# A fused attention and expert layer on one core: the buffers in on-chip memory allocated in another order, by 128-byte phase

## The chip, the cores and the metric

The kernel runs on one core of a Trainium2 chip. The metric is the device time of one execution in microseconds. The core's engines are named as in the profile: PE is TensorE (matmul), PEld its weight loads, DVE is VectorE, ACT is ScalarE, POOL is GpSimd, SP is SyncE, which issues the DMAs.

## The reference: what is computed

For a batch of 8 sequences of 1024 tokens with 256 channels:

```
# attention
qkv = x @ Wqkv + bqkv;  q, k, v = split(qkv)
q2 = (q - mean(q))**2;  q2 = q2 / (sum(q2) + 1e-7);  q2 = l2norm(q2, channels)
k2 = (k - mean(k))**2;  k2 = k2 / (sum(k2) + 1e-7);  k2 = l2norm(k2, tokens)
kv = einsum('bnc,bnd->bcd', k2, v)
t2 = einsum('bnc,bcd->bnd', q2, kv) / sqrt(N)
x  = layernorm(x + (v + t2) @ Wln + bln)
# experts: 16 experts of 128 hidden channels, all of them for every token
sel    = sigmoid(einsum('bsd,ed->bse', x, expert_sel))
scores = relu(einsum('bsd,edh->bseh', x, keys))
x  = layernorm(x + einsum('bseh,ehv,bse->bsv', scores, values, sel))
```

All of it is float32.

## The kernel before

**Precision.** An operand of a large product is kept as two tensors of the type float32r, a high part (`_h`) and a low part (`_l`). `product` makes one product from three matmuls, high by high, high by low, and low by high. In the profile all of these have line L956.

**Tiling.** Tokens go in 8 tiles of 128 for each batch element, in two halves of four tiles (512 tokens). A step belongs to one expert and one half, so there are 32 steps for each batch element, and 256 in all. In each step PE does, in this order:

- *up*: `up_bank`, hidden scores of one expert for 512 tokens. Six matmuls with 512 columns. Stationary are slices of `keys_h` and `keys_l`; moving are slices of `x1T_h` and `x1T_l` (the layer's middle result, transposed).
- what the tables `LOOP`, `FIRST` and `LAST` plan for this step, from the attention of the next batch element: *QK* (`qk_bank`, six matmuls of 512 columns, stationary `xT`, moving `wqk`), *GG* (`g_bank`, six of 256, stationary `x_h`/`x_l`, moving `k2_h`/`k2_l`), *Y* (`ring_bank`, twelve of 256, stationary `xT` and `qT`, moving `wvl` and `kvw`), *KV* (twelve of 256, stationary `gT`, which is the same memory as `k2_h`/`k2_l`, moving `wvl`), *LG* (four of 512, stationary `esel`, moving `x1T`), the transposes *QT* and *XT* (stationary `q2` or `x1`, moving `ident`, 128 columns) and the small sums *KS*.
- *down*: `down_bank`, the product with `vals`, for the gated scores of the step before. Twelve matmuls of 256 columns, stationary slices of `gated_h`/`gated_l`, moving `vals_h`/`vals_l`.

DVE makes `gated` from `up_bank` (L932) and its low part (L938), ACT the high part. The order on every engine is written out in the kernel; nothing reorders it.

**Memory.** `sb(...)` (L136 on) allocates a tensor in the on-chip memory. The allocator places tensors one behind another in the order of the calls, each rounded up to a multiple of 32 bytes per partition. All matmul operands are float32 or float32r, so 4 bytes a column. Inside a tensor, the slices that matmuls read begin at multiples of 512 bytes, so the address of a slice modulo 128 is that of its tensor. This remainder is called *phase* here.

Of the kernel before, what the change touches and what calls it, by code (L numbers as in the profile page):

```python
# [6 lines left out]
F32R = mybir.dt.float32r  # L7
# [4 lines left out]
P = 128  # L12
B, N, C = 8, 1024, 256
E, H = 16, 128
M = C // P
T = N // P
GT = 4
GN = GT * P
G = T // GT
STEPS = G * E  # L20
LAG = 1
WARM = 14
LOW = 32
EPS_SUM = 1e-7
EPS_NORM = 1e-12
# [98 lines left out]
def build_program(nc, x, xT, wqk, wvT, wln, b_qk, b_v, b_ln, esel, keys, values, ident_in, out):  # L124
    with ExitStack() as ctx:
        def sb(name, shape, dt=F32):
            return ctx.enter_context(nc.sbuf_tensor(name, shape, dt))
# [4 lines left out]
        def sem(name):  # L132
            return ctx.enter_context(nc.semaphore(name))


        keys_h, keys_l = sb("keys_h", [P, E, M, H], F32R), sb("keys_l", [P, E, M, H], F32R)  # L136
        vals_h, vals_l = sb("vals_h", [P, E, C], F32R), sb("vals_l", [P, E, C], F32R)
        wqk_h, wqk_l = sb("wqk_h", [P, M, 2 * C], F32R), sb("wqk_l", [P, M, 2 * C], F32R)
        wvl_h, wvl_l = sb("wvl_h", [P, M, C], F32R), sb("wvl_l", [P, M, C], F32R)

        esel_h, esel_hl = sb("esel_h", [P, M, P], F32R), sb("esel_hl", [P, M, P], F32R)
        qk_bias = sb("qk_bias", [P, 2 * C])
        bvl = sb("bvl", [P, C])
        out_bias = sb("out_bias", [P, C])
        ident = sb("ident", [P, P])
        ones = sb("ones", [P, P])
        eps_ln = sb("eps_ln", [P, 1])


        x_raw = sb("x_raw", [P, T, C])  # L150
        xT_raw = sb("xT_raw", [P, M, GN])
        xT_h, xT_l = sb("xT_h", [P, G, M, GN], F32R), sb("xT_l", [P, G, M, GN], F32R)
        x_h, x_l = sb("x_h", [P, 2, C], F32R), sb("x_l", [P, 2, C], F32R)
        qk = sb("qk", [P, 2 * C])
        q2 = sb("q2", [P, T, C])
        q_sum, q4_sum, q_root, q_floor, q_scale = (sb(n, [P, T]) for n in (
            "q_sum", "q4_sum", "q_root", "q_floor", "q_scale"))
        q4_lifted = sb("q4_lifted", [P, T])
        k2, k4 = sb("k2", [P, 2, C]), sb("k4", [P, C])
        k_sum, k_sum_eps, k_scale = (sb(n, [P, 2]) for n in ("k_sum", "k_sum_eps", "k_scale"))  # L160
        k2_h, k2_l = sb("k2_h", [P, 2, C], F32R), sb("k2_l", [P, 2, C], F32R)
        k2_total, k4_total = sb("k2_total", [P, C]), sb("k4_total", [P, C])
        col_sums = sb("col_sums", [P, 4, 2])
        col_norm, col_scale = sb("col_norm", [P, M, 2]), sb("col_scale", [P, M, 2])
        gT_h, gT_l = k2_h, k2_l
        kvw_h, kvw_l = sb("kvw_h", [P, M, C], F32R), sb("kvw_l", [P, M, C], F32R)
        qT_h, qT_l = sb("qT_h", [P, 2, 2, M, P], F32R), sb("qT_l", [P, 2, 2, M, P], F32R)
        y = sb("y", [P, 2, C])
        y_stats, y_mv = sb("y_stats", [P, 2, 6]), sb("y_mv", [P, 2, 2])
        y_std, y_rstd = sb("y_std", [P, 2]), sb("y_rstd", [P, 2])  # L170
        kvw = y
        x1 = sb("x1", [P, T, C])
        x1T_h, x1T_l = sb("x1T_h", [P, G, M, GN], F32R), sb("x1T_l", [P, G, M, GN], F32R)


        sel = sb("sel", [E, GN])
        sel_rows = sb("sel_rows", [P, E // 4, GN])
        sel_all = sb("sel_all", [P, 2, GN])
        gated = sb("gated", [P, GN])
        gated_h, gated_l = sb("gated_h", [P, 2, GN], F32R), sb("gated_l", [P, 2, GN], F32R)  # L180
        w_room = sb("w_room", [P, WPIECE])
        z = sb("z", [P, 2, 2, C])
        z_stats, z_mv = sb("z_stats", [P, 2, 2, 6]), sb("z_mv", [P, 2, 2, 2])
        z_std, z_rstd, z_shift = (sb(n, [P, 2, 2]) for n in ("z_std", "z_rstd", "z_shift"))


        w_stage = [w_room[:], z[:].rearrange("p a t c -> p (a t c)")]
# [2 lines left out]
        wqk_flat = wqk_raw.rearrange("p m a c -> p (m a) c")  # L190
        wqk_hi_flat = wqk_h[:].rearrange("p m (a c) -> p (m a) c", a=2)
        wqk_lo_flat = wqk_l[:].rearrange("p m (a c) -> p (m a) c", a=2)
        minus_mean, bias_mean = sb("minus_mean", [P, 2 * M]), sb("bias_mean", [P, 2])
        bqk_raw = sel_all[:, 0].rearrange("p (a c) -> p a c", a=2)
        bln_raw = y[:, 1]
        bv_col = sb("bv_col", [P, M])
        bv_wide = y[:, 0].rearrange("p (m n) -> p m n", m=M)
        table_ahead = sb("table_ahead", [P, 2])
        esel_raw = sb("esel_raw", [P, M, E])


        up_bank = [bank("up_bank0"), bank("up_bank1")]
# [60 lines left out]
        def at_least(eng, sm, count):  # L263

            if not isinstance(count, int) or count > 0:
                eng.wait_ge(sm, count)
# [20 lines left out]
        def ring_of(it, s, kind, a):  # L287
            rep = it if isinstance(it, int) else 1
            return ring_bank[RING_AT[(rep, s, kind, a)] % 2]
# [194 lines left out]
        def _(act):  # L484
            def copy(dst, src, **kw):
                return nc.scalar.activation(dst, src, ACT.Copy, **kw)  # L486
# [78 lines left out]
            def late(it, s):  # L565
# [6 lines left out]
                for kind, a, off in transposed_first(  # L572
# [32 lines left out]
                    elif kind == "LG":  # L605
# [5 lines left out]
                        at_least(act, sel_spread, b * STEPS + a * E - (E - 1))  # L611
                        copy(sel[:], ring_of(it, s, kind, a)[LOW:LOW + E, :]).then_inc(logits_low, 1)
                    elif kind == "ZN":
# [32 lines left out]
        def _(dve):  # L646
# [34 lines left out]
            def wvl_esel_lo():  # L681
# [8 lines left out]
                dve.wait_ge(esel_hi, 1)  # L690
                V.tensor_tensor(esel_hl[:, :, LOW:LOW + E], esel_raw[:], esel_h[:, :, 0:E].bitcast(F32),
                                ALU.subtract).then_inc(esel_lo, 1)
# [254 lines left out]
        def _(pe):  # L947
# [31 lines left out]
            pe.wait_ge(constants_set, 4)  # L979
            for n in range(WARM):  # L980
                mm(ring_bank[n % 2][:, 0:M * P], ones[:], esel_h[:].bitcast(F32).rearrange("p m n -> p (m n)"),  # L981
# [174 lines left out]
```

## Time and profile before

| | |
|---|---|
| median of 3 runs | 1044.8 us (1041.42 to 1045.15) |
| profiled execution, own time | 1044.54 us |
| its span in the trace | 1042.7 us |
| PE busy | 1019.5 us, 98% |
| PEld busy | 924.3 us, 89% |
| DVE busy | 796.7 us, 76% |
| ACT busy | 509.3 us, 49% |
| POOL busy | 220.1 us, 21% |
| mean DMA traffic | 31 GB/s |

The span runs from the first to the last instruction; the own time holds about 1.8 us around it. A matmul's duration in the profile holds its latency through the array, so durations of neighbours overlap, and their sum is far above the time that passes; how fast PE goes is read from starts, or from the chain that ended last, which follows PE from start to start and merges matmuls of one kind (x12 is twelve of them).

### The profile page before, as it was taken

The page shows a single profiled execution, that of the slowest core. Times are in us where ns is not written, and L with a number is a line of the kernel's source. Part 1 is how long each engine was busy: PE and PEld are TensorE (multiplying, and loading weights), DVE is VectorE, ACT ScalarE, POOL GpSimd, SP SyncE. Part 2 cuts the span into 40 slices and gives each one's busy share as a digit, 9 for nine tenths or more (in the row PEclk, how much of TensorE's full clock was granted, in tenths as well). Part 3 has the DMA queues.
Part 4 walks back from the last instruction along what each step waited for, and adds up shares of the span by engine and source line. Part 5 has one row for each costly group of instructions (what it writes and reads, how often), then busy time and mean ns, then how long its engine had stood idle before and what let it go on. Part 6 is the DMA issues. An engine that isn't in the chain of part 4 may idle for free.

```text
span 1042.7 us, 18409 instructions
## 1 busy us (share of the span) xinstructions
PE 1019.5 (98%) x6664; PEld 924.3 (89%) x6664; DVE 796.7 (76%) x1818; ACT 509.3 (49%) x1192; POOL 220.1 (21%) x273
## 2 busy tenths in 40 slices
PE   7789999999999999999999999999999999999997
PEld 6669899988999899998999989998999988999986
DVE  7779786878778787778877778677786878877565
ACT  6555653455534654356534565245643455434332
POOL 2111122212222122221222122221121211221221
PEclk9889999999999999999999999999999999999999
DMA  5032000110002000110001100011000200000000
GB/s 179 21 102 82 2 22 1 63 41 3 21 13 72 20 2 22 42 61 2 2 21 43 61 3 21 1 53 51 2 22 1 83 21 3 22 2 21 2 21 21
DMA packets 12122, 32.59 MB, mean 31 GB/s; under 512 B 1792, under 2 KB 2048, under 8 KB 12032
## 3 DMA queue, kind: packets, MB, share of 16 engines
q1 hardware_dynamic: 12032, 31.42, 9.0%
q8 instruction: 53, 0.87, 0.3%
q14 instruction: 37, 0.30, 0.1%
HBM read 22.50 MB, written 8.39 MB: 30 GB/s over the span
## 4 chain that ended last, share of the span: by engine, by line
PE 96%; DVE 3%; ACT 1%; issue 1%; POOL 0%; ACTq 0%; POOLq 0%
PE down_bank L956 34%; PE up_bank L956 34%; PE ring_bank L956 10%; PE qk_bank L956 8%; PE g_bank L956 4%; PE ring_bank L1044 1%; PE ring_bank L1060 1%; PE ring_bank L981 1%; PE ring_bank L1069 1%; PE ring_bank L1070 1%; PE ring_bank L1025 1%; DVE keys_l L909 0%; DVE k_l L852 0%; DVE qk L720 0%; DVE k_total L849 0%
## 5 line engine op out<-in xcount | busy, mean ns | idle before, releaser
L486 ACT ACTIVATE gated_h<-gated 128x512 fp32r<-128x512 f32 x256 | 161.4, 630 | 403.2 <-DVE gated L932 403.2
L472 POOL PARTITION_BROADCAST sel_all<-sel_rows x240 | 197.0, 821 | 710.2 <-DVE gated L932 709.5
L956 PE MATMUL down_bank<-vals_h,gated_h 128*128 128x256 f32 x1024 | 291.9, 285 | 0.9 <-DVE gated_l L938 0.8
L956 PE MATMUL down_bank<-vals_l,gated_h 128*128 128x256 f32 x1024 | 285.2, 279 | 0.0
L956 PE MATMUL down_bank<-vals_h,gated_l 128*128 128x256 f32 x1024 | 285.2, 279 | 0.0
L932 DVE SCALAR_TENSOR_TENSOR gated<-up_bank,sel_all 128x512 f32<-128x512 f32 x256 | 176.1, 688 | 63.0 <-PE up_bank L956 61.7
L938 DVE TENSOR_TENSOR gated_l<-gated,gated_h 128x512 fp32r<-128x512 f32 x256 | 173.3, 677 | 43.5 <-ACT gated_h L486 42.5
L956 PE MATMUL up_bank<-x1T_h,keys_l 128*128 128x512 f32 x512 | 202.4, 395 | 0.0
L956 PE MATMUL up_bank<-x1T_l,keys_h 128*128 128x512 f32 x512 | 201.9, 394 | 0.0
L956 PEld LDWEIGHTS down_bank<-vals_h,gated_h 128*128 128x128 f32 x1024 | 193.2, 189 | 9.3 <-DVE gated_l L938 3.2
L956 PE MATMUL up_bank<-x1T_h,keys_h 128*128 128x512 f32 x512 | 201.2, 393 | 0.0
L956 PEld LDWEIGHTS down_bank<-vals_l,gated_h 128*128 128x128 f32 x1024 | 192.9, 188 | 4.6
L956 PEld LDWEIGHTS down_bank<-vals_h,gated_l 128*128 128x128 f32 x1024 | 192.7, 188 | 0.0
L956 PEld LDWEIGHTS up_bank<-x1T_h,keys_l 128*128 128x128 f32 x512 | 96.7, 189 | 20.4
L956 PEld LDWEIGHTS up_bank<-x1T_l,keys_h 128*128 128x128 f32 x512 | 96.8, 189 | 11.5
L956 PEld LDWEIGHTS up_bank<-x1T_h,keys_h 128*128 128x128 f32 x512 | 96.7, 189 | 11.1
L720 DVE TENSOR_TENSOR qk<-qk_bank,qk_bias 128x512 f32<-128x512 f32 x60 | 41.3, 689 | 35.9 <-PE qk_bank L956 35.8
L733 DVE TENSOR_TENSOR y<-ring_bank,x_raw 128x256 f32<-128x256 f32 x64 | 27.0, 423 | 32.9 <-PE ring_bank L956 32.9
L956 PE MATMUL qk_bank<-wqk_h,xT_h 128*128 128x512 f32 x120 | 49.1, 409 | 0.0
L956 PE MATMUL qk_bank<-wqk_h,xT_l 128*128 128x512 f32 x120 | 47.4, 395 | 0.0
L956 PE MATMUL qk_bank<-wqk_l,xT_h 128*128 128x512 f32 x120 | 47.3, 394 | 0.0
L486 ACT ACTIVATE k_h<-k,k_scale 128x256 fp32r<-128x256 f32 x64 | 32.6, 509 | 27.8 <-DVE k_scale L767 27.1
(158 smaller groups left out, 1682.0 us busy)
## 6 DMA issues: line engine op xcount, KB each, us to landing
xT_raw<-in_xT SPq DMA_DIRECT2D x16, 512.0 KB, 4.0
x_raw<-in_x SPq DMA_DIRECT2D x16, 512.0 KB, 4.6
out<-z SPq DMA_DIRECT2D x32, 256.0 KB, 2.3
w_room<-in_keys SPq DMA_DIRECT2D x4, 512.0 KB, 4.3
z<-in_values SPq DMA_DIRECT2D x4, 512.0 KB, 3.8
sel_rows<-sel SPq DMA_DIRECT2D x64, 8.0 KB
x<-in_wqk SPq DMA_DIRECT2D x1, 512.0 KB, 3.6
sel_all<-in_b_qk SPq DMA_DIRECT2D x1, 256.0 KB, 5.1
```

The costliest lines, as they stand in the source:

```text
L472: nc.gpsimd.partition_broadcast(sel_all[:, e % 2], row, P).then_inc(sel_spread, 1)
L486: return nc.scalar.activation(dst, src, ACT.Copy, **kw)
L720: V.tensor_tensor(qk_of(it, t)[:], qk_bank_of(it, t)[:], qk_bias[:], ALU.add).then_inc(qk_biased, 1)
L733: V.tensor_tensor(y[:, a % 2], ring_of(it, s, "Y", a)[:, 0:C], x_raw[:, a], ALU.add).then_inc(y_added, 1)
L932: V.scalar_tensor_tensor(out=gated[:], in0=up_bank[s % 2][:], scalar=0.0, in1=sel_all[:, s % 2], op0=ALU.max, op1=ALU.mult).then_inc(gate_ ...
L938: V.tensor_tensor(gated_l[:, s % 2], gated[:], gated_h[:, s % 2].bitcast(F32), ALU.subtract).then_inc(gated_lo, 1)
L956: last = mm(dst, lhs, rhs, start=start and i == 0, stop=stop and i == n - 1, **kw)
L981: mm(ring_bank[n % 2][:, 0:M * P], ones[:], esel_h[:].bitcast(F32).rearrange("p m n -> p (m n)"), start=True, stop=True)
L1025: last = mm(bk[:, j:j + 2], total[:, m * P:(m + 1) * P], ones[:, 0:2], start=True, stop=True)
L1044: last = nc.tensor.transpose(bk[:, j:j + P], q2[:, 2 * a + i, m * P:(m + 1) * P], ident[:])
L1060: last = nc.tensor.transpose(bk[:, m * P:(m + 1) * P], x1[:, a, m * P:(m + 1) * P], ident[:])
L1069: mm(bk[:], esel_hl[:, m], x1T_h[:, a, m], start=(m == 0), stop=False)
```

## The change

The `sb` calls stand in another order. Moving operands come first, then 64 bytes that nothing uses (`half_line`), then stationary operands, then everything that no matmul reads, with small tensors (under 128 bytes) at the end. No shape, no instruction and no wait is changed; on each engine the same instructions stand in the same order, and only the addresses in them differ. The core of the diff:

```diff
+LINE = 128
...
-        keys_h, keys_l = sb("keys_h", [P, E, M, H], F32R), sb("keys_l", [P, E, M, H], F32R)
         vals_h, vals_l = sb("vals_h", [P, E, C], F32R), sb("vals_l", [P, E, C], F32R)
+        x1T_h, x1T_l = sb("x1T_h", [P, G, M, GN], F32R), sb("x1T_l", [P, G, M, GN], F32R)
         wqk_h, wqk_l = sb("wqk_h", [P, M, 2 * C], F32R), sb("wqk_l", [P, M, 2 * C], F32R)
         wvl_h, wvl_l = sb("wvl_h", [P, M, C], F32R), sb("wvl_l", [P, M, C], F32R)
...
+        kvw_h, kvw_l = sb("kvw_h", [P, M, C], F32R), sb("kvw_l", [P, M, C], F32R)
+        k2_h, k2_l = sb("k2_h", [P, 2, C], F32R), sb("k2_l", [P, 2, C], F32R)
+        gT_h, gT_l = k2_h, k2_l
+        ident, ones = sb("ident", [P, P]), sb("ones", [P, P])
+
+
+        half_line = sb("half_line", [P, LINE // 8])
+        keys_h, keys_l = sb("keys_h", [P, E, M, H], F32R), sb("keys_l", [P, E, M, H], F32R)
+        gated_h, gated_l = sb("gated_h", [P, 2, GN], F32R), sb("gated_l", [P, 2, GN], F32R)
         xT_h, xT_l = sb("xT_h", [P, G, M, GN], F32R), sb("xT_l", [P, G, M, GN], F32R)
         x_h, x_l = sb("x_h", [P, 2, C], F32R), sb("x_l", [P, 2, C], F32R)
+        qT_h, qT_l = sb("qT_h", [P, 2, 2, M, P], F32R), sb("qT_l", [P, 2, 2, M, P], F32R)
+        esel_h, esel_hl = sb("esel_h", [P, M, P], F32R), sb("esel_hl", [P, M, P], F32R)
+        q2, x1 = sb("q2", [P, T, C]), sb("x1", [P, T, C])
+        k2_total, k4_total = sb("k2_total", [P, C]), sb("k4_total", [P, C])
```

Phases (address modulo 128) in the two built programs, moving / stationary, for each kind of product:

| product | matmuls in one batch element | before | after |
|---|---|---|---|
| up: `x1T` / `keys` | 192 of 512 columns | 64 / 0 | 0 / 64 |
| down: `vals` / `gated` | 384 of 256 | 0 / 64 | 0 / 64 |
| QK: `wqk` / `xT` | 48 of 512 | 0 / 32 | 0 / 64 |
| GG: `k2` / `x_h`, `x_l` | 48 of 256 | 64 / 32 | 0 / 64 |
| Y, first half: `wvl` / `xT` | 48 of 256 | 0 / 32 | 0 / 64 |
| Y, second half: `kvw` / `qT` | 48 of 256 | 32 / 32 | 0 / 64 |
| KV: `wvl` / `gT` | 12 of 256 | 0 / 64 | 0 / 0 |
| LG: `x1T` / `esel` | 8 of 512 | 64 / 0 | 0 / 64 |
| transposes: `ident` / `q2`, `x1` | 32 of 128 | 0 / 32, 0 / 64 | 0 / 64 |

## Rows read from the trace of the kernel before

**Rows 1.** The page: busy time by engine, and slices of PE and its clock.
```profile
PE 1019.5 (98%) x6664; PEld 924.3 (89%) x6664; DVE 796.7 (76%) x1818; ACT 509.3 (49%) x1192; POOL 220.1 (21%) x273
...
PE   7789999999999999999999999999999999999997
...
PEclk9889999999999999999999999999999999999999
```

**Rows 2.** The page: the chain that ended last, by engine.
```profile
PE 96%; DVE 3%; ACT 1%; issue 1%; POOL 0%; ACTq 0%; POOLq 0%
```

**Rows 3.** Stretches of one batch element: us, busy of PE, PEld, DVE, ACT, POOL (instructions), clock, DMA.
```profile
287.00:412.00 125.00, 125.00 (x833) 113.95 (x833) 97.92 (x226) 62.48 (x148) 26.41 (x33) 1.00 0.08 27
412.00:537.00 125.00, 125.00 (x833) 113.95 (x832) 97.87 (x227) 62.48 (x148) 26.34 (x32) 1.00 0.08 27
```

**Rows 4.** PE's waits, 100 to 1036 us: in total, times, longest.
```profile
PE down_bank L956 <- DVE gated_l L938: 0.8, 1, 0.8
```

**Rows 5.** The chain in order of time, 442 to 566.7 us: start, length, what.
```profile
442.00 1.50 PE down_bank L956 x12
443.51 1.40 PE up_bank L956 x6
444.91 1.42 PE ring_bank L956 x12
446.33 1.36 PE down_bank L956 x12
447.69 1.37 PE up_bank L956 x6
449.06 1.39 PE down_bank L956 x12
...
466.44 1.41 PE down_bank L956 x12
467.85 1.40 PE up_bank L956 x6
...
469.47 1.40 PE qk_bank L956 x6
470.87 1.42 PE down_bank L956 x12
472.28 1.40 PE up_bank L956 x6
473.69 0.70 PE g_bank L956 x6
474.39 1.42 PE down_bank L956 x12
475.80 1.40 PE up_bank L956 x6
...
563.07 0.44 PE ring_bank L1044 x4
563.50 1.39 PE down_bank L956 x12
564.89 1.37 PE up_bank L956 x6
```

**Rows 6.** The chain a little later, 479 to 505 us.
```profile
483.00 1.40 PE qk_bank L956 x6
484.39 1.38 PE down_bank L956 x12
485.77 1.37 PE up_bank L956 x6
487.14 0.71 PE g_bank L956 x6
```

**Rows 7.** The longest pieces of the whole chain that repeat once a batch element.
```profile
566.70 1.50 PE down_bank L956 x12
...
691.40 1.50 PE down_bank L956 x12
```

More of the change, by code:

```diff
@@ L133, in sem @@
             return ctx.enter_context(nc.semaphore(name))
-        keys_h, keys_l = sb("keys_h", [P, E, M, H], F32R), sb("keys_l", [P, E, M, H], F32R)
         vals_h, vals_l = sb("vals_h", [P, E, C], F32R), sb("vals_l", [P, E, C], F32R)
+        x1T_h, x1T_l = sb("x1T_h", [P, G, M, GN], F32R), sb("x1T_l", [P, G, M, GN], F32R)
         wqk_h, wqk_l = sb("wqk_h", [P, M, 2 * C], F32R), sb("wqk_l", [P, M, 2 * C], F32R)
         wvl_h, wvl_l = sb("wvl_h", [P, M, C], F32R), sb("wvl_l", [P, M, C], F32R)
-        esel_h, esel_hl = sb("esel_h", [P, M, P], F32R), sb("esel_hl", [P, M, P], F32R)
@@ L142, in build_program @@
[L142 to L151, printed above, removed]
+        kvw_h, kvw_l = sb("kvw_h", [P, M, C], F32R), sb("kvw_l", [P, M, C], F32R)
+        k2_h, k2_l = sb("k2_h", [P, 2, C], F32R), sb("k2_l", [P, 2, C], F32R)
+        gT_h, gT_l = k2_h, k2_l
@@ L154, in build_program @@
+        esel_h, esel_hl = sb("esel_h", [P, M, P], F32R), sb("esel_hl", [P, M, P], F32R)
+        q2, x1 = sb("q2", [P, T, C]), sb("x1", [P, T, C])
+        k2_total, k4_total = sb("k2_total", [P, C]), sb("k4_total", [P, C])
+        x_raw, xT_raw = sb("x_raw", [P, T, C]), sb("xT_raw", [P, M, GN])
+        qk_bias = sb("qk_bias", [P, 2 * C])
+        bvl, out_bias = sb("bvl", [P, C]), sb("out_bias", [P, C])
         qk = sb("qk", [P, 2 * C])
-        q2 = sb("q2", [P, T, C])
-        q_sum, q4_sum, q_root, q_floor, q_scale = (sb(n, [P, T]) for n in (
-            "q_sum", "q4_sum", "q_root", "q_floor", "q_scale"))
@@ L158, in build_program @@
-        q4_lifted = sb("q4_lifted", [P, T])
         k2, k4 = sb("k2", [P, 2, C]), sb("k4", [P, C])
[L160 to L165, printed above, removed]
@@ L166, in build_program @@
-        kvw_h, kvw_l = sb("kvw_h", [P, M, C], F32R), sb("kvw_l", [P, M, C], F32R)
-        qT_h, qT_l = sb("qT_h", [P, 2, 2, M, P], F32R), sb("qT_l", [P, 2, 2, M, P], F32R)
         y = sb("y", [P, 2, C])
-        y_stats, y_mv = sb("y_stats", [P, 2, 6]), sb("y_mv", [P, 2, 2])
-        y_std, y_rstd = sb("y_std", [P, 2]), sb("y_rstd", [P, 2])
         kvw = y
-        x1 = sb("x1", [P, T, C])
-        x1T_h, x1T_l = sb("x1T_h", [P, G, M, GN], F32R), sb("x1T_l", [P, G, M, GN], F32R)
         sel = sb("sel", [E, GN])
@@ L179, in build_program @@
         gated = sb("gated", [P, GN])
-        gated_h, gated_l = sb("gated_h", [P, 2, GN], F32R), sb("gated_l", [P, 2, GN], F32R)
         w_room = sb("w_room", [P, WPIECE])
         z = sb("z", [P, 2, 2, C])
+        eps_ln = sb("eps_ln", [P, 1])
+        q_sum, q4_sum, q_root, q_floor, q_scale = (sb(n, [P, T]) for n in (
+            "q_sum", "q4_sum", "q_root", "q_floor", "q_scale"))
+        q4_lifted = sb("q4_lifted", [P, T])
+        k_sum, k_sum_eps, k_scale = (sb(n, [P, 2]) for n in ("k_sum", "k_sum_eps", "k_scale"))
+        col_sums = sb("col_sums", [P, 4, 2])
+        col_norm, col_scale = sb("col_norm", [P, M, 2]), sb("col_scale", [P, M, 2])
+        y_stats, y_mv = sb("y_stats", [P, 2, 6]), sb("y_mv", [P, 2, 2])
+        y_std, y_rstd = sb("y_std", [P, 2]), sb("y_rstd", [P, 2])
         z_stats, z_mv = sb("z_stats", [P, 2, 2, 6]), sb("z_mv", [P, 2, 2, 2])
         z_std, z_rstd, z_shift = (sb(n, [P, 2, 2]) for n in ("z_std", "z_rstd", "z_shift"))
+        minus_mean, bias_mean = sb("minus_mean", [P, 2 * M]), sb("bias_mean", [P, 2])
+        bv_col, esel_raw = sb("bv_col", [P, M]), sb("esel_raw", [P, M, E])
+        table_ahead = sb("table_ahead", [P, 2])
         w_stage = [w_room[:], z[:].rearrange("p a t c -> p (a t c)")]
@@ L192, in build_program @@
         wqk_lo_flat = wqk_l[:].rearrange("p m (a c) -> p (m a) c", a=2)
-        minus_mean, bias_mean = sb("minus_mean", [P, 2 * M]), sb("bias_mean", [P, 2])
         bqk_raw = sel_all[:, 0].rearrange("p (a c) -> p a c", a=2)
         bln_raw = y[:, 1]
-        bv_col = sb("bv_col", [P, M])
         bv_wide = y[:, 0].rearrange("p (m n) -> p m n", m=M)
-        table_ahead = sb("table_ahead", [P, 2])
-        esel_raw = sb("esel_raw", [P, M, E])
         up_bank = [bank("up_bank0"), bank("up_bank1")]
```

## The prediction

> **What bounds the kernel now.** I read the page first. PE is busy for 98% of the span, DVE for 76%, the rest far less [rows 1], and the chain that ended last is PE for 96% of its length, DVE for 3% [rows 2]. In the stretches of one batch element PE is busy for all of the 125 us at full clock, 2.4 GHz [rows 3]. From 100 to 1036 us PE waits for another engine only once, for 0.8 us [rows 4]. So outside the first 66 us or so nobody holds PE up, and its time is the sum of the distances from one matmul's start to the next.
>
> These distances are in the chain. Pure streaming at 2.4 GHz would take 256/2.4 = 106.7 ns for a matmul of 256 columns and 213.3 ns for one of 512, so 1.28 us for a group of twelve down matmuls and also for a group of six up matmuls. The chain shows neither. It shows two paces: a quick one, 1.36 us for down and 1.37 us for up (446.33 and 447.69), and a slow one, 1.42 us and 1.40 us (470.87 and 472.28, 474.39 and 475.80) [rows 5]. Per matmul that is 113 or 118 ns for 256 columns, and 228 or 233 ns for 512. Same instructions, same shapes, same addresses modulo 128, no wait in either. Of the 32 down groups between 442.0 and 566.7 us, 20 take 1.36 to 1.39 us, eleven 1.41 or 1.42, and one, behind a transpose, 1.50; the 32 together are 44.68 us. Of the 32 up groups, 21 take 1.37 or 1.38 and eleven 1.40; together 44.18 us. The pace carries over from a group to the next: 470.87 to 475.80 is slow in all of its up and down groups, 446.33 to 447.69 quick [rows 5]. One period is 124.70 us, 566.70 to 691.40 [rows 7], and there are close to eight of them in the span, so a microsecond per period is worth 8 us.
>
> **The change part by part.** No instruction is added, removed or moved, on any engine or queue. What can change is how long PE takes to read its operands, and how long the others take to read and write theirs.
>
> *Products whose phases differ by 32 or 0 now and by 64 after* (QK, GG, Y). In the same stretch the eight QK groups take 1.40 us each, never 1.37 [rows 5, 6]. The nine groups of twelve in the ring (eight Y and one KV) take 12.72 us, so 1.413 each, as 1.42 at 444.91 [rows 5]. The eight GG groups take 5.79 us, one of them 0.81, the others 0.70 to 0.72 [rows 5, 6]; twelve at that pace would be 1.42. So all products that are not 64 apart go at the slow pace or close to it, and those that are 64 apart, up and down, at the quick pace two times in three. I read that as a connection, though not a proven one. If the former go as up and down do on average (down 44.56/32 = 1.393 without the transposed one's extra 0.12, up 1.381), Y and KV gain 9 x 0.020 = 0.18 us, GG 8 x (0.724 - 0.697) = 0.22, QK 8 x 0.019 = 0.15: 0.55 us a period.
>
> *Up and down, 64 apart before and after.* What is left is where the slow pace starts. Behind GG, down is slow (473.69, then 474.39); behind Y it is quick (444.91, then 446.33), behind QK either (469.47 then 1.42, 483.00 then 1.38) [rows 5, 6]. If GG and QK no longer stand apart, some of the eleven slow groups of each kind become quick. All of them would give 11 x 0.055 + 11 x 0.03 = 0.94 us, with the mixed groups of 1.38 and 1.39 brought to 1.36 as well 32 x 1.36 + 0.12 = 43.64 against 44.68 and 32 x 1.37 = 43.84 against 44.18, so 1.38 us. None gives 0. I take half of the 1.38, 0.7 us, as nothing says which neighbours stay slow: transposes remain, with `x1` at the phase it had.
>
> *KV* goes from 64 apart to 0 apart, the one product that goes the other way: twelve matmuls a period, at most 0.06 us a period if it is slow after, as the difference of 1.42 and 1.36. LG is only mirrored, eight matmuls a period; I put it at nothing.
>
> *Other engines.* DVE, ACT, POOL and the DMAs get other addresses too, all still multiples of 32 bytes. I cost that at nothing, because DVE has 27 us of slack in each 125 us [rows 3] and PE waits for it nowhere [rows 4]. Without cover, in the first 66 us and the last few, DVE is 3% of the chain [rows 2], 31 us; a change of one per cent in its speed would be 0.3 us.
>
> The sum is 0.55 + 0.7 - 0.06 = 1.2 us a period, times eight 9.5 us. The profiled execution's own 1044.5 us becomes 1035.0; the median of the runs is 0.3 us above it. I predict **1035 us**.
>
> The bounds of this term from rows: everything at the quick pace saves 1.38 us for up and down, 9 x 0.053 = 0.48 for the ring, 8 x (0.724 - 0.68) = 0.35 for GG and 8 x 0.03 = 0.24 for QK, 2.45 us a period, 20 us in all: **1025 us**. Everything at the slow pace costs 32 x 1.42 + 0.12 - 44.68 = 0.88 for down and 32 x 1.40 - 44.18 = 0.62 for up, 1.5 us a period: **1057 us**.
>
> **The rivals.**
>
> *Phase does not matter.* The two paces come out of the timing of the loads and matmuls alone, and come out alike. For it: the same phases show both paces [rows 5], which an address alone cannot make. Against it: QK, GG and Y never show the quick one. The time is that of before, 1044.8 us. The Trainium skill speaks for this rival, and against any gain: its page "SBUF — State Buffer", section "Who interferes with whom", gives TensorE two independent read ports, one for the moving operand and one for the weights, and says that "PE and ACT never wait on anyone". The trace agrees as to other engines, in that PE has no wait in the steady part [rows 4], but by that rule alone the chain should show one pace and not two.
>
> *The mirrored phase is worse, or everything locks at the slow pace* (the other side). Up is the only large product whose moving phase changes, from 64 to 0. The one product of 512 columns whose moving operand stands at phase 0 now, QK, takes 1.40 us in all eight groups and never 1.37 [rows 5, 6]. If that is because of its moving phase, the 21 quick up groups go to 1.40, 0.62 us a period, 5 us: 1050 us, and since the pace carries over, down would follow at 1.42, which is the 1057 us above. It decides from the point where up alone is slow, if the other products gain nothing. Against it: GG's moving operand is at 64 and is no quicker than Y's at 0.
>
> *A third pace, free of all loss.* If reading both operands at once is what keeps PE above 106.7 ns, and a distance of 64 everywhere removed it, the pace would be that of the transposes. Four of them take 0.44 us for 4 x 128 columns [rows 5], at two cycles a column 106.7 ns each, so 3.3 ns above pure streaming. One period has some 780 matmuls of the large products, whose pure streaming takes 109 us (40.96 for down, as much for up, 11.5 for the ring, 10.2 for QK, 5.1 for GG, less rounding) and which take 118.6 now (44.68 + 44.18 + 12.72 + 11.20 + 5.79); with 3.3 ns each, 2.6 us, 7 us a period would be saved, 57 us: 988 us. Against it: down and most of up already stand 64 apart, before as after, and lose 6% and more. The Trainium skill's page "TensorE: Matmul & The Clock Gate", section "Wait — 56ns, not 53.3ns?", puts back-to-back matmuls at about 2.5 ns over pure streaming, an estimate of 63 us saved; the trace's 1.37 us for six of 512 does not agree with that page, being 15 ns over for each.
>
> **How the numbers follow.** A measurement of this kernel can tell about 0.5%, 5 us, from no change. My forecast, a partial move to the quick pace (1028 to 1039), has 0.40; nearly everything quick, or quicker than that (1015 to 1028), 0.10; the third pace, 0.04; no or little effect (1040 to 1050), 0.27; the slower case (1050 to 1060), 0.19. Faster by over 0.5% sums to 0.53, with a little of the forecast's upper edge falling inside 0.5%; same 0.28; slower 0.19. The range 1022 to 1054 leaves out the third pace, part of the quick case and the worse half of the slow one, about 2 in 10. The forecast's own range is 1028 to 1039.
>
> **What would show it right or wrong.** In the chain of the changed kernel, QK groups at 1.37 to 1.38 and Y groups at 1.36 to 1.40 would show the first term, and fewer than eleven slow down groups in a period, above all behind GG, the second. Up groups all at 1.40 would show the mirrored phase to be worse. The same counts of 1.36, 1.42, 1.37 and 1.40 would show that phase does nothing. A pace that is in neither list, such as 1.31 us for up or down, would be the third. The prediction is wrong altogether if PE gets waits that it does not have now, so that DVE or a DMA was slowed, or if the two paces hang on something else in the addresses than their remainder by 128.

## The result and the profile after

The changed kernel takes 1040.66 us (median of 13 runs, 1036.8 to 1042.4) against 1044.21 us for the kernel before (13 runs beside them, 1041.12 to 1045.33). The ratio is 0.9964, with a 95% interval of 0.9952 to 0.9976: faster by 0.36%, or 3.8 us (the two medians themselves are 3.6 us apart). The forecast was 9.5 us. So the sign was right and the size was not. The time lies inside the stated range of 1022 to 1054, but outside the forecast's own range of 1028 to 1039: it falls in the band "no or little effect (1040 to 1050)", which had a chance of 0.27.

The page of the changed kernel, busy time by engine and the chain's shares (lines of the source are four lower than before):

```profile
span 1038.8 us, 18409 instructions
PE 1015.1 (98%) x6664; PEld 915.9 (88%) x6664; DVE 794.9 (77%) x1818; ACT 509.0 (49%) x1192; POOL 221.5 (21%) x273
...
PE 96%; DVE 3%; ACT 1%; issue 1%; POOL 0%; ACTq 0%; POOLq 0%
```

The span fell by 3.9 us and PE's busy time by 4.4. The weight loads' busy time fell by 8.4 us, that of DVE, ACT and POOL moved by less than 2. The counts are the same, PE is still nearly the whole chain, and its one wait from 100 to 1036 us is what it was [rows 4]:

```profile
PE down_bank L952 <- DVE gated_l L934: 0.8, 1, 0.8
```

The chain in order of time (start, length, what), first where the Y groups stand, then where GG and QK stand; the answering rows of before are [rows 5, 6]:

```profile
442.21 1.40 PE up_bank L952 x6
443.61 1.37 PE ring_bank L952 x12
444.99 1.36 PE down_bank L952 x12
446.35 1.39 PE up_bank L952 x6
447.74 1.37 PE down_bank L952 x12
...
482.77 1.36 PE down_bank L952 x12
484.14 1.40 PE up_bank L952 x6
485.53 0.69 PE g_bank L952 x6
486.22 1.40 PE qk_bank L952 x6
487.61 1.36 PE down_bank L952 x12
...
490.37 0.69 PE g_bank L952 x6
491.06 1.36 PE down_bank L952 x12
...
521.06 1.44 PE ring_bank L952 x12
```

What to see: a group of Y takes 1.37 us where it took 1.42 or 1.41, a group of GG 0.69 where it took 0.70 to 0.72, and down is at 1.36 also behind GG and QK. Of the 30 down groups directly behind GG from 150 to 990 us, all took 1.42 before, and 24 take 1.36 now, the other six 1.41; slow down groups (1.41 or 1.42) in one period fell from eleven to five. But QK still takes 1.40, and up, which took 1.37 in two groups of three, takes 1.39 or 1.40 in every one. The last row is KV, whose operands now stand at one phase: 1.44 us.

A *period* is the stretch of one batch element, some 124 us; all sums here are from the one that begins at 442 us. Over it, 32 down, 32 up, 9 ring, 8 QK and 8 GG groups as in the prediction, sums in us:

| | down | up | ring (Y, KV) | QK | GG | all five |
|---|---|---|---|---|---|---|
| before | 44.68 | 44.18 | 12.72 | 11.20 | 5.79 | 118.57 |
| after | 44.06 | 44.69 | 12.41 | 11.21 | 5.64 | 118.01 |
| difference | -0.62 | +0.51 | -0.31 | +0.01 | -0.15 | -0.56 |

Eight periods make 4.5 us of that, against 3.9 us less span. Down, the ring and GG gain 1.08 us a period together, and up takes 0.51 of it back.

### The profile page after: what moved, and what is told of

It is laid out like the page before. It is cut to its first block, busy times and chain, and to the rows that moved or that the text cites. A ratio compares the mean times of both kernels' runs of the same rounds, so it can differ in the third digit from the quotient of the medians.

```text
span 1038.8 us, 18409 instructions
## 1 busy us (share of the span) xinstructions
PE 1015.1 (98%) x6664; PEld 915.9 (88%) x6664; DVE 794.9 (77%) x1818; ACT 509.0 (49%) x1192; POOL 221.5 (21%) x273
## 4 chain that ended last, share of the span: by engine, by line
PE 96%; DVE 3%; ACT 1%; issue 1%; POOL 0%; ACTq 0%; POOLq 0%
PE up_bank L952 34%; PE down_bank L952 34%; PE ring_bank L952 10%; PE qk_bank L952 8%; PE g_bank L952 4%; PE ring_bank L1040 1%; PE ring_bank L1056 1%; PE ring_bank L977 1%; PE ring_bank L1065 1%; PE ring_bank L1066 1%; PE ring_bank L1021 1%; DVE k_l L848 0%; DVE keys_l L905 0%; DVE qk L716 0%; DVE k_total L845 0%
```

## The experiments

All of them change addresses alone: no instruction, wait or order is touched. Ratios are to runs of the kernel before beside them on the same chip, whose median was 1044.5 to 1044.9 us. Means of a group in us are over one period of one profiled execution. A function `at(phase)` puts unused room between tensors, so that the next one starts at a given address modulo 128 or 256. In what follows the *lead* of a product is the address of its stationary operand less that of its moving one, modulo 256. In the kernel before, down has lead 64, up 192, QK and the first half of Y 32, the second half of Y 0, GG 224. The changed kernel has 64 in all of them, KV (0) excepted. Transposes and small sums are left out of these tables, and *ring* is the mean of eight Y groups and the one of KV.

**1. The changed kernel, with up and LG alone turned back.**

```diff
+        at(64)
         x1T_h, x1T_l = sb("x1T_h", [P, G, M, GN], F32R), sb("x1T_l", [P, G, M, GN], F32R)
+        at(0)
         wqk_h, wqk_l = sb("wqk_h", [P, M, 2 * C], F32R), sb("wqk_l", [P, M, 2 * C], F32R)
...
-        half_line = sb("half_line", [P, LINE // 8])
+        at(0)
         keys_h, keys_l = sb("keys_h", [P, E, M, H], F32R), sb("keys_l", [P, E, M, H], F32R)
+        at(64)
         gated_h, gated_l = sb("gated_h", [P, 2, GN], F32R), sb("gated_l", [P, 2, GN], F32R)
...
+        at(0)
         esel_h, esel_hl = sb("esel_h", [P, M, P], F32R), sb("esel_hl", [P, M, P], F32R)
+        at(64)
         q2, x1 = sb("q2", [P, T, C]), sb("x1", [P, T, C])
```

> The changed kernel, but up and LG as before: x1T at phase 64, keys and esel at 0; all else as after (moving 0, stationary 64). Theory A, phase acts on each product by itself: up groups return from 1.39-1.40 us to 1.37, some 0.65 us a period or 5 us in all, while Y, GG and down keep the quick pace; about 1035 us, ratio to the kernel before 0.991. Theory B, what counts is that moving and stationary stand at the same two phases in all products, so that no transition breaks the pace: up stays at 1.40 or the slow down groups come back, 1041 to 1045 us. Theory C, the gain came from where the tensors lie and not from the phase: no difference from the changed kernel, 1040.7 us.

Measured: 1048.66 us, ratio 1.0043 (1.0031 to 1.0055). None of the three theories gave that time. Up stayed at 1.397 us a group, and down went to 1.407. Modulo 128 the phases are what I asked for. Modulo 256 they are not those of the kernel before: the room moved `gated` and `keys`, and left down with lead 192 and up with lead 64, the reverse of before.

**2. The old order with the new phases modulo 128.** Thirteen `at(0)` or `at(64)` calls in the order of before.

> The order of the kernel before, with unused room put between tensors so that every matmul operand has the phase of the changed kernel. Theories A and B, only the phase counts: as the changed kernel, 1040.7 us, up 1.39-1.40, Y 1.37, GG 0.69. Theory C, the order counts: as the kernel before, 1044.2 us, with QK, GG and Y at the slow pace and up at 1.37 in two groups of three.

Measured: 1048.35 us, 1.0031 (1.0018 to 1.0044), slower than either kernel, so neither theory holds as I put it. QK fell to 1.385 us, down was at 1.403. Down, QK, GG and the first half of Y have lead 192 here, up and the second half of Y 64. The ten runs spread from 1043.91 to 1049.72 us, and the profiled one is the quickest of them.

**3 and 4. All operands at one phase, and the changed kernel mirrored** (moving operands at 64, stationary at 0, modulo 128). The edits are `half_line` taken away, and in 4 `at(64)` ahead of `vals_h` and `at(0)` ahead of `keys_h` as well.

> The changed kernel without the 64 bytes of room: all matmul operands at phase 0. Theory A: a distance of 0 is slow for 256 columns, as KV went from 1.39 to 1.44 us in the changed kernel; all groups of twelve at 1.42 to 1.44, up 1.40 or more: 1057 to 1062 us. If the distance does nothing, 1040.7 us.

> The changed kernel mirrored: all moving operands at phase 64, all stationary ones at 0. Theory A, in the form that a phase of 64 for the moving operand is what makes 512 columns quick: up 1.37 in nearly all groups and QK 1.37 too, 0.85 us a period under the changed kernel; if 256 columns do not mind, 1034 us. In the form that each width wants its own arrangement, down, Y and GG fall back to 1.42: about 1042 to 1046 us. Theory B, only the distance of 64 counts: 1040.7 us, with up at 1.40.

Measured: 1057.3 us, 1.0123 (1.011 to 1.0136), and 1039.66 us, 0.9952 (0.9936 to 0.9968). The chain of the one with a single phase:

```profile
449.54 1.43 PE ring_bank L961 x12
450.97 1.44 PE down_bank L961 x12
452.41 1.39 PE up_bank L961 x6
453.80 1.43 PE down_bank L961 x12
```

and of the mirrored one:

```profile
442.35 1.39 PE up_bank L963 x6
443.74 1.37 PE down_bank L963 x12
445.11 1.39 PE up_bank L963 x6
446.50 1.37 PE ring_bank L963 x12
447.87 1.36 PE down_bank L963 x12
```

So phase acts: 17.6 us, or 1.7%, lie between these two layouts. And the distance between the two operands counts while mirroring the two sides does not: in the mirrored version `x1T` stands at 192 modulo 256, where the kernel before has it, and up is still at 1.397. A moving phase of 0 is not what slows up or QK.

**5 and 6. Room of 192 and of 128 bytes in place of 64.** `at(0)` ahead of `vals_h`, and `at(192)` or `at(128)`, modulo 256, in place of `half_line`.

> The changed kernel with 192 bytes of room in place of 64 (and 128 more ahead of everything): modulo 128 the phases are those of the changed kernel, 0 and 64; modulo 256 the stationary operands stand 192 ahead of the moving ones instead of 64. Theory A of phases modulo 128: as the changed kernel, 1040.7 us, groups of twelve at 1.36-1.37, up 1.39-1.40. Theory D, what counts is the lead, the stationary address less the moving one, modulo 256: products of 256 columns slow (down 1.41, Y 1.41, GG 0.70-0.71), those of 512 quicker (up 1.37-1.38, QK 1.38); down and ring lose 41 x 0.04, GG 0.1, up and QK gain 40 x 0.02, in all +0.9 us a period, 1048 us.

> The changed kernel with 128 bytes of room in place of 64: modulo 128 all operands at one phase, modulo 256 the stationary ones 128 ahead of the moving ones. Theory A, modulo 128: as the version with all operands at one phase, 1057 us, groups of twelve at 1.43-1.44. Theory D, modulo 256: a lead that no run has shown so far, so another pace than 1.43, up or down.

Measured: 1040.18 us, 0.9971 (0.9956 to 0.9987), and 1055.41 us, 1.011 (1.0091 to 1.0129). With 192 the total is that of the changed kernel, as modulo 128 would have it, but it is made of other parts. Two places in its chain:

```profile
442.26 1.36 PE down_bank L963 x12
443.62 1.37 PE up_bank L963 x6
...
447.73 1.36 PE ring_bank L963 x12
...
489.60 1.37 PE up_bank L963 x6
490.97 1.37 PE qk_bank L963 x6
492.34 1.41 PE down_bank L963 x12
493.76 1.37 PE up_bank L963 x6
495.13 0.71 PE g_bank L963 x6
```

Up is at 1.37 in both places, 1.375 on average, and QK at 1.37 for the first time. That part of theory D came in as forecast. Down and the ring have both paces at this lead, 1.36 and 1.41; I had forecast the slow one alone. With 128, no down, ring or GG group is quick (down 1.426, ring 1.428, GG 0.722 on average).

**7. Each width at its own lead.** Stationary at 64, moving operands of 256 columns at 0 and of 512 columns at 128, modulo 256.

```diff
+        at(0)
         vals_h, vals_l = sb("vals_h", [P, E, C], F32R), sb("vals_l", [P, E, C], F32R)
+        at(128)
         x1T_h, x1T_l = sb("x1T_h", [P, G, M, GN], F32R), sb("x1T_l", [P, G, M, GN], F32R)
...
+        at(0)
         wvl_h, wvl_l = sb("wvl_h", [P, M, C], F32R), sb("wvl_l", [P, M, C], F32R)
...
-        half_line = sb("half_line", [P, LINE // 8])
+        at(64)
```

> All stationary operands at 64 modulo 256, moving operands of 256-column products at 0 (lead 64), moving operands of 512-column products, x1T and wqk, at 128 (lead 192). Theory D: every width at the pace that is best for it so far, down 1.36-1.38, Y 1.37, GG 0.69, up 1.37, QK 1.38; against the changed kernel 32 x 0.025 + 8 x 0.02 = 0.95 us a period, 7.6 us in all: 1033 us, ratio to the kernel before 0.989. Theory A, modulo 128, where it has the same phases as the changed kernel: 1040.7 us.

Measured: 1049.06 us, 1.0053 (1.0038 to 1.0067). Its chain:

```profile
448.23 1.41 PE down_bank L965 x12
449.64 1.39 PE up_bank L965 x6
...
453.83 1.41 PE ring_bank L965 x12
```

A clear miss. Down and Y have the lead of 64 at which they run at 1.36 in the changed kernel, and go at 1.41. Leads that are good in a uniform layout do not add up.

**8. The old order with the new phases modulo 256.**

> The order of the kernel before, with room that gives every matmul operand the phase of the changed kernel modulo 256 (moving 128, stationary 192), though not modulo 512. Theory D: as the changed kernel, 1040.7 us, ratio 0.996, down 1.36-1.38, Y 1.37, GG 0.69, up and QK 1.40. If the order or larger distances count (theory C): down and Y at 1.40 or more, as in the version with the old order and phases modulo 128 alone, 1048 us.

Measured: 1039.67 us, 0.996 (0.9949 to 0.9972); down 1.383, up 1.394, ring 1.378, QK 1.40, GG 0.705. This is the changed kernel in all its parts; the largest difference is 0.006 us, in down. So the order of the tensors and their distances beyond 256 bytes did nothing that these runs can tell; where they stand within 256 bytes did. Together with run 2, which has the same order and the same phases modulo 128, it also shows that 128 is too short a period: 128 bytes here and there made 8.7 us.

**9, 10 and 11. The parts of the change by themselves.** Phases are modulo 256 here. In 9, up, LG and down stand as in the kernel before, the rest as in the changed one. In 10, only up and LG are mirrored in the kernel before; every other tensor keeps its address modulo 256, those that no matmul reads included. In 11, QK gets lead 192 on top of 9. The edit of 10:

```diff
+        at(192)
         keys_h, keys_l = sb("keys_h", [P, E, M, H], F32R), sb("keys_l", [P, E, M, H], F32R)
+        at(128)
         vals_h, vals_l = sb("vals_h", [P, E, C], F32R), sb("vals_l", [P, E, C], F32R)
...
+        at(128)
         x1T_h, x1T_l = sb("x1T_h", [P, G, M, GN], F32R), sb("x1T_l", [P, G, M, GN], F32R)
...
```

> Up, LG and down exactly as in the kernel before, by phases modulo 256 (x1T 192, keys and esel 128, vals 128, gated 192), and Y, GG and QK as in the changed kernel (moving 128, stationary 192). This is the part of the change other than the mirrored up, without the shift by 128 that the first attempt at it had. If the parts add up: Y and GG quick (1.37, 0.69 us), up at 1.381 or better, down at 1.396 or better since GG no longer leaves the slow pace behind; from 1037 us, if only Y and GG gain, to 1030 us, if up and down are quick throughout. If the pace of down and up depends on which phases stand next to each other rather than on their own: down at 1.41, up at 1.39-1.40, 1047 to 1049 us, as in the two other mixed arrangements.

> The kernel before, with up and LG alone mirrored (x1T from 192 to 128, keys and esel from 128 to 192, modulo 256). If the mirrored up is what took back part of the gain: up from 1.381 to 1.397 us a group, 0.5 us a period, 4 us in all, 1048 us, and Y, GG and QK as in the kernel before. If the slower up of the changed kernel came from its new neighbours instead: up stays at 1.38, 1044 us.

> As the first of these four, with wqk at 0 modulo 256, so that QK too has its stationary operand 192 ahead. If a lead of 192 is what is quick for 512 columns: QK from 1.40 to 1.37-1.38 us, 0.2 us a period, 1.6 us less than the first one. If the mixed arrangement sets a slow rhythm: 1047 to 1049 us.

Measured: run 9 1041.49 us, 0.9972 (0.9958 to 0.9987); run 10 1047.27 us, 1.002 (1.0003 to 1.0036); run 11 1044.86 us, 1.0003 (0.9989 to 1.0016). The mirrored up alone costs up nearly what it was charged with, 1.381 to 1.394 us a group. It also changes the pace of down, whose own addresses stay: of the 30 down groups behind GG (150 to 990 us) 24 go from 1.42 to 1.37 or 1.38 us, and of the 28 directly behind Y or KV 27 go from 1.36 to 1.41. The answering rows of before are in [rows 5]; here are those of run 10:

```profile
450.62 1.42 PE ring_bank L972 x12
452.04 1.41 PE down_bank L972 x12
...
472.59 0.70 PE g_bank L972 x6
473.29 1.37 PE down_bank L972 x12
```

Without the mirrored up, in run 9, up keeps 1.380, and all 30 down groups behind GG take 1.36, but the ring then reaches only 1.404 and GG 0.720 where the changed kernel has 1.379 and 0.705, and down 1.389 against 1.377. So the change cannot be split into a good part and a bad one: leaving up alone saves 0.54 us a period in up and gives 0.75 back in the others. In 11 QK gains 0.1 us a period, and up and down lose 0.6.

**12 to 15. The leads between.** Uniform layouts as in the changed kernel, with 32, 96, 160 and 224 bytes, modulo 256. The room moves everything behind it as well, tensors included that only the other engines use; PE waits for none of them from 100 us on in these runs, but no run varies their addresses alone.

> The changed kernel with 32 bytes of room in place of 64: all stationary operands 32 ahead of the moving ones. If a lead of 32 is why QK, GG and Y were slow in the kernel before: groups of twelve at 1.41-1.42 throughout, GG 0.71-0.72, up and QK 1.40: 1053 to 1057 us. If only the meeting of different phases was: 1040.7 us.

> All stationary operands 96 ahead of the moving ones, modulo 256. If only leads of 64 and 192 are quick for 256 columns: groups of twelve at 1.42, as at a lead of 32, 1054 to 1057 us. If the pace falls with the distance from 64: between 1041 and 1056 us.

> All stationary operands 160 ahead. If only 64 and 192 are quick: 1054 to 1057 us, groups of twelve at 1.42, up 1.39-1.40. If a lead between 128 and 192 is quicker for 512 columns than 192 is: up under 1.375.

> All stationary operands 224 ahead, which is what QK and the first half of Y had in the kernel before. If only 64 and 192 are quick: 1054 to 1057 us, groups of twelve at 1.42, up and QK at 1.40 as QK was before.

(The text for 224 ahead is mistaken in one point: QK and the first half of Y had lead 32 in the kernel before, and it was GG that had 224.) All uniform layouts, with the mean of a group over one period in us (KV, one group of the ring's nine, has lead 0 in every row):

| lead | down (12 of 256) | ring | GG | up (6 of 512) | QK | median us | ratio |
|---|---|---|---|---|---|---|---|
| 0 | 1.434 | 1.434 | 0.725 | 1.390 | 1.375 | 1057.3 | 1.0123 |
| 32 | 1.422 | 1.422 | 0.728 | 1.399 | 1.397 | 1056.19 | 1.0116 |
| 64 (the change) | 1.377 | 1.379 | 0.705 | 1.397 | 1.401 | 1040.66 | 0.9964 |
| 96 | 1.418 | 1.419 | 0.720 | 1.404 | 1.405 | 1056.72 | 1.0111 |
| 128 | 1.426 | 1.428 | 0.722 | 1.392 | 1.391 | 1055.41 | 1.011 |
| 160 | 1.440 | 1.440 | 0.726 | 1.403 | 1.404 | 1061.33 | 1.0167 |
| 192 | 1.397 | 1.383 | 0.715 | 1.375 | 1.375 | 1040.18 | 0.9971 |
| 224 | 1.405 | 1.406 | 0.714 | 1.397 | 1.396 | 1050.3 | 1.0049 |

For 256 columns 64 is the quickest lead and 192 the second; a lead of 224 is between these and the rest, where the expectation of run 15 had 1054 to 1057 us. For 512 columns 192 is the quickest, with 0 as quick for QK alone, and none between is better. The mixed layouts beside them:

| | down | ring | up | QK | median us |
|---|---|---|---|---|---|
| before: leads 64, mixed, 192, 32 | 1.396 | 1.413 | 1.381 | 1.400 | 1044.21 |
| run 1: 192, 64, 64, 64 | 1.407 | 1.380 | 1.397 | 1.397 | 1048.66 |
| run 2: 192, mixed, 64, 192 | 1.403 | 1.397 | 1.394 | 1.385 | 1048.35 |
| run 7: 64, 64, 192, 192 | 1.412 | 1.412 | 1.389 | 1.380 | 1049.06 |
| run 9: 64, 64, 192, 64 | 1.389 | 1.404 | 1.380 | 1.402 | 1041.49 |
| run 10: 64, mixed, 64, 32 | 1.392 | 1.419 | 1.394 | 1.401 | 1047.27 |
| run 11: 64, 64, 192, 192 | 1.401 | 1.397 | 1.386 | 1.390 | 1044.86 |

In all runs up is at 1.39 or more at every lead but 192, and at 1.375 to 1.389 at 192.

## Why the prediction was right in sign and wrong in size

**What bounds the kernel** held: from 100 us on no wait came or went between before and after, and the difference lies in PE's distance from start to start, in paces that up and down showed before the change too.

**"Products whose phases differ by 32 or 0 now and by 64 after"** was right for Y and GG, and Y was undersized: ring 0.31 us a period measured, KV's loss included (1.39 to 1.44, as forecast in kind), where the sum had 0.18 less 0.06. GG gave 0.15 for 0.22. (Of the mirrored rival the text says that up is the only large product whose moving phase changes; those of GG and of the second half of Y change too.) It was wrong for QK: 0.15 us forecast, nothing found. The reason is that I took the distance of 64 as one thing for all widths, on the strength of up and down. But modulo 256 up had lead 192 and down 64, and the table shows that these are not alike: at 64 QK takes 1.401, at 192 1.375. With its three parts taken together this term was nearly right: 0.45 us a period, KV's loss included, for 0.49.

**"Up and down, 64 apart before and after"** is the step that failed. It said that these products could only gain, by half of 1.38 us, since they stood 64 apart before as after. Down did gain, 0.62 us, and where it was expected, behind GG. But the reason given, that GG would no longer stand apart, is not the only thing that does it: in run 10 GG stands as before, and 24 of 30 down groups behind it are quick all the same. Up was not left where it was: mirroring it turned its lead from 192 to 64 modulo 256, and it lost 0.51 us. The step's 0.7 came out as 0.11, which is 4.7 us of the 5.7 by which forecast and measurement differ; that it was half of 1.38 was a choice, as the text says, with no row for it. Run 10 shows this loss by itself (up from 1.381 to 1.394), and runs 4 and 8 show it with the others' gains in place.

**The right sign was in part luck.** Run 2 has every phase that the prediction reckoned with, modulo 128, and takes 1048.35 us, more than the kernel before. That the order chosen gave all products the lead of 64 modulo 256, and no mixture, was not in the reasoning.

**The other side's rival**, a worse mirrored phase, named the right product and nearly the right price (0.62 us a period for up; 0.51 measured), but not the cause: it blamed the moving operand's phase of 0. Run 4 has it at 64 modulo 128 and up is as slow. It also had down follow up into the slow pace, which it did not in the changed kernel. **"Phase does not matter"** is refuted by 1040 against 1057 us for 64 bytes of room or none. The Trainium skill's page "SBUF — State Buffer", section "Who interferes with whom", by which the loads of weights and the moving operand have ports of their own and PE waits for nobody, does not lead one to expect these 17 us. **The third pace** is in no layout: no group of twelve of 256 or six of 512 columns took less than 1.36 us. Its two cycles a column for the transposes are a reading of their 110 ns, which are 2.06 cycles of 2.4 GHz a column.

**Doubts named at the end** proved right: the two paces do hang on something else in the addresses than the remainder by 128. The evidence was in the two programs' addresses, which I had read modulo 128 only.

**What stays open.** Why the lead acts at all, and why mixed layouts fall short of their parts. Run 7 and the kernel before give up and down the same leads, 192 and 64, and differ in what stands next to what when PE goes from a product to the next: `vals` and `keys` at the same address modulo 256 before, 64 apart in run 7. Down takes 1.412 us in the one, 1.396 in the other. Runs 7 and 11 have the same lead in every product, and are 4 us apart. Run 10 shows that a group's pace depends on what ran before it, and not on its neighbour alone: with up mirrored, down changes its pace behind GG and behind Y, though neither it nor they have moved within 256 bytes (all have moved by multiples of 256, which did nothing in run 8). That the crossings, or the moment at which a stream restarts behind a transpose, choose the pace is an idea that fits these rows; no run isolates it. A crossing of 64 between `vals` and `keys` cannot be the whole of it, since the changed kernel has one too, and down takes 1.377 us there.

No layout beats the changed kernel by more than the measurement can tell: run 4 at 0.9952 (0.9936 to 0.9968) and run 8 at 0.996 overlap with its 0.9964 (0.9952 to 0.9976).

## What to carry to other kernels

When PE is busy throughout and no wait is left, compare the distances between starts of like matmuls with the columns divided by the clock, and look for two paces in one kind of group; here 2% lay between the best and the worst layout (1039.66 and 1061.33 us), and 0.5% between the kernel before and the best, at no cost in instructions. Try a few uniform layouts of moving against stationary operands, in steps of 32 bytes over at least 256, and measure them, since a period of 128 misled both the prediction and the first two experiments. Giving each product the lead that suited it in a uniform layout made this kernel slower (run 7, 1049.06 us).

## What the runs showed of the hardware that I had not expected

A matmul of float32r with 256 columns takes 113 to 120 ns from start to start at full clock according to where its operands stand in 256 bytes (1.36 to 1.44 us for twelve), with the same instructions and no waits.

The pace of a stream of matmuls is carried on. In run 10 the order, the waits and all addresses modulo 256 but those of up and LG are the same as before, and down, two groups further on, changes from 1.36 to 1.41 us behind Y and from 1.42 to 1.37 behind GG.

Runs of one kernel differ by 4 to 6 us, and those with a higher mean clock are the quick ones: the changed kernel took 1036.8 and 1037.34 us at a mean granted clock of 0.994, and 1039.68 to 1042.4 at 0.986 to 0.991. Two profiled executions show where. That of the mirrored version (run 4) has a span of 1034.9 us, 3.9 less than that of the changed kernel, though one period's sum is the same in both (117.98 and 118.01 us). From 16 to 66 us (length, PE's busy time and matmuls, clock, DMA share, GB/s) the changed kernel has

```profile
16.00:66.00 50.00, 35.64 (x180) 0.83 0.10 36
```

and the mirrored version has

```profile
16.00:66.00 50.00, 36.63 (x204) 0.90 0.15 50
```

In this stretch PE is busy for 36 of 50 us; the rest goes in waits, nearly all for DVE, in the first half-filled steps. The granted clock was 0.83 of full in the one execution and 0.90 in the other, with 24 more matmuls done in the same 50 us. At the steady pace of 833 matmuls in 125 us [rows 3], 24 matmuls are 3.6 us, nearly all of the 3.9. Whether the clock made the lead or only went with it is not shown. For a change of this size one profiled execution is not enough: the medians of several runs say what its parts are worth, and the chain within one period says where.
